# The routed-expert rows of the second block prepared one step later in the shared expert, one division moved behind a product, and weight loads issued in one run

## The reference, cut to what matters

```python
def _expert(h, g, u, d):                       # I = 704 hidden channels
    return einsum('...i,hi->...h', silu(h @ g.T) * (h @ u.T), d)
x = x + xattn(layernorm(x), ctx, ctx, mask)    # block 2, attention, 16 heads
h = layernorm(x)
out = _expert(h, sg, su, sd)                   # shared expert
probs = softmax(h @ wr.T + rb)
scores, idx = top_k(probs, 2)                  # then normalised to sum 1
for e in range(7):
    out = out + w[..., e] * _expert(h, rg[e], ru[e], rd[e])
x = x + out
```

## Time and profile before

| | us |
|---|---|
| median of 3 runs | 511.58 |
| lowest, highest | 511.38, 511.62 |
| the profiled execution, its own time | 511.38 |
| its span in the profile | 510.1 |
| TensorE busy | 490.9 (96%) |
| VectorE busy | 259.0 (51%) |
| ScalarE busy | 201.4 (39%) |
| mean granted TensorE clock | 0.991 of full |

### The profile page before, as it was taken

The page is one execution under the profiler, slowest core; times in us unless marked ns, Lnnn a source line. Parts: engine busy times, 40 slices in busy tenths (PEclk is TensorE's granted clock), DMA queues, the critical chain, the costliest instruction groups (busy, mean ns, idle before and its releaser), DMA issues.

```text
span 510.1 us, 8828 instructions
## 1 busy us (share of the span) xinstructions
PE 490.9 (96%) x3293; PEld 369.9 (73%) x3293; DVE 259.0 (51%) x776; ACT 201.4 (39%) x416; POOL 85.7 (17%) x124
## 2 busy tenths in 40 slices
PE   6999999999999999999999999999999999999994
PEld 4555545648999987655655366666899999999993
DVE  4678897664465654886669453512222222222210
ACT  2747556452537445345556622211222222222221
POOL 2246100004030300200000000470022122121122
PEclk9999999999999999979999999999999999999999
DMA  8820009996132310290000030387886676686612
GB/s 294 245 65 6 2 0 340 366 364 201 42 95 73 103 32 22 70 341 1 2 1 2 13 112 1 90 300 223 265 260 216 197 260 210 194 268 196 210 22 27
DMA packets 43384, 73.13 MB, mean 143 GB/s; under 512 B 3554, under 2 KB 33730, under 8 KB 43333
## 3 DMA queue, kind: packets, MB, share of 16 engines
q1 hardware_dynamic: 34580, 60.47, 35.9%
q0 software_dynamic: 4336, 6.75, 6.0%
q10 hardware_dynamic: 4416, 5.26, 3.2%
HBM read 56.35 MB, written 14.51 MB: 139 GB/s over the span
## 4 chain that ended last, share of the span: by engine, by line
PE 83%; DVE 9%; DMA 4%; ACT 1%; issue 1%; ACTq 0%; POOL 0%; DVEq 0%; POOLq 0%
PE PS L2007 17%; PE PS L2022 9%; PE PS L890 9%; PE PS L1916 8%; PE PS L900 6%; PE PS L1789 5%; PE PS L402 5%; PE PS L1802 5%; PE PS L921 4%; PE PS L1927 3%; DVE W L1093 3%; PE PS L376 2%; PE PS L909 2%; DMA CT<-in_ctxT 2%; PE PS L381 1%; DMA VR<-scratch_rows 1%
## 5 line engine op out<-in xcount | busy, mean ns | idle before, releaser
L1093 DVE TENSOR_REDUCE W<-PS 128x2 f32<-128x512 f32 x128 | 83.7, 686 | 34.9 <-PE PS L890 34.1
L2007 PE MATMUL PS<-PR,W 128*128 128x128 f32 x836 | 96.5, 275 | 0.0
L2007 PEld LDWEIGHTS PS<-PR,W 128*128 128x128 f32 x836 | 94.9, 192 | 0.1
L890 PE MATMUL PS<-W 32*128 32x256 f32 x512 | 84.4, 404 | 2.2 <-DVE W L1093 1.8
L900 PE MATMUL PS<-W 32*128 32x512 f32 x256 | 78.8, 647 | 0.2
L890 PEld LDWEIGHTS PS<-W 32*128 32x128 f32 x512 | 56.2, 187 | 24.9 <-issue 10.9
L2022 PE MATMUL PS<-W,PR 128*128 x228 | 52.5, 380 | 0.8 <-ACT PR L2740 0.8
L2791 POOL DMA_INDIRECT out<-PR,slots x19 | 29.7, 1563 | 134.5 <-ACT PR L2740 131.4
L1260 ACT ACTIVATE PR<-PS 128x512 f32<-128x512 f32 x64 | 35.2, 595 | 32.2 <-PE PS L900 32.1
L2022 PEld LDWEIGHTS PS<-W,PR 128*128 128x128 f32 x228 | 41.9, 190 | 6.1 <-issue 1.2
L2043 DVE TENSOR_TENSOR PR<-PR,PS 128x512 f32<-128x512 f32 x19 | 13.1, 687 | 59.9 <-PE PS L2007 59.9
(11 more groups left out here) (274 smaller groups left out, 618.6 us busy)
## 6 DMA issues: line engine op xcount, KB each, us to landing
W<-in_rguT SPq DMA_DIRECT2D x19, 1408.0 KB, 6.2
W<-in_L_ffn_W SPq DMA_DIRECT2D x16, 512.0 KB, 9.7
W<-in_rdT SPq DMA_DIRECT2D x5, 768.0 KB, 10.8
scratch_rows<-W SPq DMA_DIRECT2D x1, 2860.0 KB, 15.1
VR<-scratch_rows SPq DMA_DIRECT2D x19, 130.0 KB, 5.5
W<-in_mask SPq DMA_DIRECT2D x2, 1024.0 KB, 12.3
scratch_x<-W SPq DMA_DIRECT2D x1, 2048.0 KB, 14.6
PR<-scratch_x SPq DMA_DIRECT2D x16, 128.0 KB, 2.3
```

The costliest lines, as they stand in the source:

```text
L890: m = pe.matmul(PS[:, bank, q * FK:(q + 1) * FK], QT[r:r + 32, g, c:c + 128], KT[r:r + 32, g, b * FK:(b + 1) * FK], start=True, stop=True)
L1093: dve.tensor_reduce(NM[:, s % 2, q:q + 2, c], PS[:, m_bank(use), :].rearrange("p (q n) -> p q n", q=2), AX, ALU.max).then_inc(sem("m_free" ...
L2007: m = pe.matmul(PS[:, bank, j * 128:(j + 1) * 128], W[:, o:o + 128], XS[:, r % 2, k, :], start=(k == 0), stop=(k == 1))
```

## The change

Three things are written otherwise. In `beside1` the turning of batch 1's rows, their logits with the choice of experts, and gates, ranks and places go from steps 2, 3 and 4 to steps 3, 4 and 5; the tile table stays in step 5 and now follows the places directly. ScalarE's copy of the turned rows moves likewise; its Exp for the gates stays at step 4. The division of head group 6's outputs goes from ahead of the shared expert to behind the first product. SyncE no longer holds the second weight load back until the eighth product, nor the third until the rows' loads are issued: all three go out in a row.

```diff
 def beside1(n):                  # TensorE
-            elif n == 2:
+            elif n == 3:
                 pe.wait_ge(*at(1, "rows", 8))
                 turn_batch("rows1_1", rows_for(1, 1))
-            elif n == 3:
+            elif n == 4:
                 taken(6, "rows1_1")
                 claim(7, "logits1_1")
                 filled(7, logits_pe(1, 4, 4, 7))
-            elif n == 4:
+            elif n == 5:
                 claim(7, "ranks1")
                 filled(7, ranks_pe(2))
...
 def beside1(n):                  # VectorE
             if n == 0:
+                dve_divide(1, 6, v)
                 dve_divide(1, 7, v)
                 add_outputs(v, 1)
                 whole(statistics(v, "rows1_1", rows_of(1)))
...
-            elif n == 2:
+            elif n == 3:
                 dve_xt("rows1_1", 1)
-            elif n == 3:
+            elif n == 4:
                 dve.wait_ge(*full(7, "logits1_1"))
                 freed(7, logits_dve(1, 4, 4, 7))
                 dve.wait_ge(*full_free(7, "logits1_1"))
                 whole(choose_experts(v, 2))
-            elif n == 4:
+            elif n == 5:
                 gates1(v)
                 dve.wait_ge(*full(7, "ranks1"))
                 whole(places1(v, full_free(7, "ranks1")))
-            elif n == 5:
                 whole(tables1(v))
-        dve_divide(1, 6, v)
         shared_dve(beside1)
...
 def beside1(n):                  # ScalarE
-            elif n == 2:
+            elif n == 3:
                 act_xt("rows1_1", (6,), 1)
             elif n == 4:
                 gates_act(2)
...
-            load_up(0)
-            sp.wait_ge(sem("mul"), CHUNKS - 4)
-            load_up(1)
+            for r in range(UPS):
+                load_up(r)
             sp.wait_ge(sem("scattered"), SCATTERED[2])
             load_x(0)
             load_x(1)
-            load_up(2)
```

## The result

| | before | changed |
|---|---|---|
| time, us, median (lowest to highest, executions) | 511.58 (509.88 to 514.03, 13) | 513.96 (513.20 to 517.53, 13) |
| ratio to before, 95% interval | 1 | 1.0065 (1.005 to 1.0082) |
| time of the profiled execution | 511.38 | 517.48 |
| its span | 510.1 | 516.2 |
| TensorE busy in the span | 490.9 (96%) | 491.3 (95%) |

The change costs 2.4 us by the medians and 3.3 (2.6 to 4.2) by the ratio. TensorE does no more work than before, it waits. The profiled execution of the changed kernel is 3.5 us above the median of its kernel, so its profile holds something that most executions don't; a second profile of the same kernel (experiment e5: 514.77 us, span 513.5) shows which part that is. The record of the changed kernel has 46 executions in all: 28 between 513.0 and 515.4 us, 16 between 515.7 and 516.6, and two at 517.5.

What follows compares the result with a forecast made beforehand. The prediction took TensorE's own queue as the bound, so its new waits add to the time: 1.5 + 1.4 + 2.7 - 0.8 = +4.8 us, giving 516.3 us, with a range of 513.6 to 519.8.

Steps and rivals of the forecast that it cites:

- The bound: From 284 us on, TensorE's own queue is the path, so everything it newly waits for is added to the time.
- Step A: Division of group 6 behind the first product: TensorE's transposes for group 7 start late, +1.5 us (1.3 to 1.7).
- Step B: Choice one step later: first scatter 8.9 us later, at 332.4; `shared_down(6)` waits for the sums, +1.4 us (1.0 to 2.0).
- The drain: Skill rule of about 1.38 us per ScalarE table switch; left out of the sum, would give some 517.7 us.
- Step C: Last scatter issued into full DMA queues, landing in 4.9 us: TensorE waits 2.7 us for tile 0's rows (0.5 to 4.8).
- the quiet bound: Lower bound for the last scatter's landing, 2.7 us from issue, giving a wait of 0.5 us at tile 0.
- Tile 2: Routed tile 2: the 0.83 us wait for its rows should go, -0.8 us (0 to -1.1).
- The half clock: Rival: the wait before dense routed matmuls drops TensorE's clock to half, 3.4 us more, 519.7 us; chance 0.13.
- the quiet end: Rival: weight loads finish early beside the scatters, tile 0 costs 0.5 us and not 2.7, 514.1 us; chance 0.18.
- The prediction's own case: All terms together, +4.8 us, 516.3 us with its own range of 515 to 518; chance 0.53.
- three signs: Wrong if first scatter before 330, last lands in under 3 us, or clock below full between 330 and 370.

Runs made afterwards that it cites:

- e5: The changed kernel itself, run and profiled again: median 513.94 us against 512.15 before, ratio 1.0028; profiled execution 514.77 us.
- e3: The kernel before with only the division of head group 6 moved behind the first product: 513.95 us against 511.87, ratio 1.0047.
- e7: The changed kernel with ScalarE's Exp for the gates moved from step 4 to step 5, behind the short Silu: 514.01 us against 512.15 before, ratio 1.0058.
- e11: The changed kernel with one more 1408 KB transfer on SyncE's queue behind the three weight loads: 520.45 us (one execution) against 511.68 before.
- e8: The kernel before with ScalarE's last two down-weight loads issued behind the Silu of routed tiles 2 and 3: 511.40 us against 512.15, ratio 0.9982.
- e2: The changed kernel with SyncE's edit undone, so the old order of weight loads: 517.43 us against 511.87 before, ratio 1.0127.
- e9: The changed kernel with SyncE's edit undone, run once more on another chip: 519.58 us against 511.68 before, ratio 1.0141.
- e6: The changed kernel without the sixteen scatters of the second block, routed tiles working on empty rows: 515.06 us (one execution) against 512.15 before.
- e10: The kernel before with SyncE's edit and ScalarE's last two down-weight loads moved behind tiles 2 and 3: 512.10 us against 511.68, ratio 1.0009.
- e1: The kernel before with only SyncE's edit, three weight loads in one run: 512.11 us against 511.87, ratio 1.0012.

## Why the prediction was right in sign, and high

- **The bound.** Right: every new wait of TensorE came out as time. Behind the shared expert's start 3.1 us of waits are 3.1 us of time in e5.
- **Step A**, +1.5: the idle time is 1.57, the start of `shared_up(1)` 1.76 later. e3 has it alone.
- **Step B**, first scatter at 332.4 and +1.4: the scatter starts at 332.26, TensorE is idle for 0.96, and between `shared_up(1)` and `shared_up(7)` it falls 1.31 behind (3.07 - 1.76; 0.11 of that in front of the wait, where the turning stands elsewhere in the stream). The sums end at 335.23 where 335.6 was worked out. The reading that the Silu behind the Exp makes the scatters later by more than the step (5.2) and the division (1.5) was right: they came 8.7 later, and in e7, with the Exp behind the Silu, 2.0 earlier than in e5.
- **The drain** of 1.38 us that the Trainium skill (ScalarE: Activation LUTs, What ACT_TABLE_LOAD costs) puts on a switch isn't in the trace: the load at 325.36 takes 1.28 and the Silu starts at 326.65. With such a drain the first scatter would, by an estimate from the page's figure, have come at about 333.6.
- **Step C**, +2.7: the term that failed. Measured 0.31 in e5, and 0 in the first profile, where the hold had made TensorE late. The last scatter was issued on time (351.31 and 351.81, forecast 351.5), and landed in 2.7, the quiet bound, where 4.9 was taken. The error is the work worked out for the engines: 4.5 us of data time for a weight load, as 6.7 less 2.2 for a transfer's fixed part. At the 413 GB/s of e5 a load of 1408 KB is 3.5 us, and a scatter (2.13 MB on GpSimd's queue for the sixteen) 0.3. Three loads and 14.5 scatters (5.8 us at the 0.4 of the prediction) are then 10.5 + 4.7 = 15.2 us behind 337.3, so 352.5, and not 356.6. The trace has the fall of the DMA share at 352 to 354. And e11, which adds 1.4 MB, brings the late scatter (5.9) and the wait (3.92) back. What a single DMA takes from issue to landing less a small transfer's time is not its share of the engines when several queue up.
- **Tile 2**, -0.8: it did not go. The rows come 0.46 late at tile 2 in e5, 0.59 at a later tile in the first profile. The prediction put the lateness down to the third weight load and took it that ScalarE's loads, starting by tile 0, would not matter. e8 shows that they do: without them the rows take 1.9 us for 7.0 (6.5 in e5).
- **SyncE's edit.** The prediction costed it within the whole and never asked what the kernel would be without it. e2 and e9 against e5 show that it saves 3.5 and 5.6 us there by the medians (the latter across two chips), 1.0 (without the hold) and 4.5 in the traces.
- **The half clock** rival had a mechanism that exists and a price twice too high: 1.71 us where 3.4 was taken from the stretch of the earlier trace rows. That reading was right for its execution (the clock was down from 221 to 228), but the same stretch in e5 lost 1.70 (222 to 226). The half clock came true in the slower profile, behind a wait that the prediction didn't have. The Trainium skill (TensorE: Matmul & The Clock Gate, What's actually happening) says that the throttled clock is the default and that activity releases it; the traces agree in so far as waits of 1.92, 3.34 and 3.92 us were each followed by the 1.2 GHz level, and those of 0.2 to 1.70 in this stretch (1.70 in e6) by none.
- **The sum.** 516.3 was forecast. 1.76 + 1.31 and about 0 for the rows on 511.58 give 514.6, against 513.96 measured: inside the range, 0.4 above its lower end of 513.6, and nearest to the rival of the quiet end at 514.1, which had a chance of 0.18. The prediction's own case, with 515 to 518 and a chance of 0.53, did not come. (Its terms' bounds, +1.7 to +8.5, would also give 513.3 to 520.1, a little more than the stated range.) Part of the hit is luck: 2.4 us too much at tile 0 was partly made up by 0.8 too much gain at tile 2.
- **Its own signs.** Of the three signs by which the prediction said it would be wrong, the first scatter kept to its side (332.26, not before 330). The last scatter landed in 2.7, under 3, in both profiles, and the clock fell to 0.50 between 358 and 361 in the first profile, though not in e5. By its own measure it was right in sign and in steps A and B, and wrong in step C.

## What to carry to other kernels

An instruction moved behind one that waits is paid in full if the engine that bounds the kernel waits for it, even though its own engine is half idle; read the idle time in front of the neighbour, not the engine's busy share. An edit's worth depends on the others: late scatters made early weight loads worth 3.5 us by the medians that had been worth nothing. When several transfers queue up, add their bytes at the rate of full queues (413 GB/s here) to find when the engines are done, and not their single times from issue to landing.

## What the runs showed of the hardware

- Sixteen DMA engines with three weight loads and sixteen row scatters in their queues moved 413 to 414 GB/s; one scatter took 2.7 us from issue to landing in the emptying queues and about 6 in full ones (5.9 in e11).
- A wait of TensorE of 1.92, 3.34 or 3.92 us in front of dense matmuls (the changed kernel, e9, e11) is followed by three to four microseconds below full clock, and the loss was 1.71 us each time, whatever the wait. Waits of 1.46 in e2 and 1.70 in e6 were not; behind the one of e2:

```profile
374.00:376.00 2.00, 1.98 (x18) 1.98 (x19) 0.42 (x1) 0.00 (x0) 1.53 (x1) 1.00 0.99 409
```

- A load of 130 KB of rows took 1.9 us (e8) and 2.1 (e10) from issue to landing without ScalarE's down weights beside it, and 5.5 to 9.2 with them (5.5 in the first profile of the changed kernel, 5.7 in e1, 6.5 in e5, 7.0 before, 7.9 in e6, 9.2 in e9).
- ScalarE and VectorE can stand for 2 to 5.5 us longer than usual in front of an instruction whose input is ready, in some executions and not in others of the same kernel. All of these fell in or just behind the stretch of full DMA queues; that these cause it isn't shown.
